# Moving half of the int4 compares to ScalarE and the mean-of-magnitudes sums to VectorE

## The reference, cut to what matters

```python
def simulate_quantize_int4(w):                 # layer 0, kernel: [1024, 1024]
    scale = jnp.max(jnp.abs(w)) / INT4_QMAX    # INT4_QMAX = 7.0
    q = jnp.clip(jnp.round(w / scale), -8.0, 7.0)
    return q * scale
...
def _quantize(W):                              # layer 1, W1 and W2
    gamma = jnp.mean(jnp.abs(W))
    return jnp.clip(jnp.round(W / (gamma + EPS)), -1.0, 1.0)
...
xn = _layernorm(x, axis=-1)
x = x + _L0_attn_ref(xn, ...) + _L0_ffn_ref(xn, kernel, bias, a, b)
xn = _layernorm(x, axis=-1)
x = x + _L1_attn_ref(xn, ...) + _L1_ffn_ref(xn, W1, b1, W2, b2)
```

## Time and profile before

| | us |
|---|---|
| median of 2 runs (1529.71 to 1533.32) | 1531.51 |
| the profiled execution | 1530.7 |
| its span on the slowest core, core 6 | 1529.2 |
| spans of the 8 cores | 1512.2 to 1529.2 |

### The profile page before, as it was taken

The page is one execution under the profiler, slowest core; times in us unless marked ns, Lnnn a source line. Parts: engine busy times, 40 slices in busy tenths (PEclk is TensorE's granted clock), DMA queues, the critical chain, the costliest instruction groups (busy, mean ns, idle before and its releaser), DMA issues. The chain is left out here.

```text
span 1529.2 us, 15301 instructions; the slowest of 8 cores (1512.2 to 1529.2 us)
## 1 busy us (share of the span) xinstructions
PE 1226.1 (80%) x5332; PEld 532.6 (35%) x5440; DVE 418.0 (27%) x704; ACT 474.2 (31%) x550; POOL 140.3 (9%) x184
## 2 busy tenths in 40 slices
PE   0277169999797587674559999999997999999997
PEld 0022024444343233221224444444443444444443
DVE  0498345002323323333167300030002200141000
ACT  0564023435424536626113241014102140032400
POOL 2341100000110211202200000000000000000000
PEclk9988679999898898896769999999998999999999
DMA  9796773002435637657592452355235152252432
GB/s 202 106 169 112 102 118 56 1 1 90 124 90 195 189 118 243 204 186 210 135 189 38 149 153 85 111 195 151 95 110 193 42 152 83 83 193 76 118 110 110
DMA packets 74202, 194.42 MB, mean 127 GB/s; under 512 B 8272, under 2 KB 16496, under 8 KB 69776
## 3 DMA queue, kind: packets, MB, share of 16 engines
q0 software_dynamic: 37072, 105.34, 28.4%
q1 hardware_dynamic: 37056, 88.09, 18.4%
HBM read 195.57 MB, written 33.56 MB: 150 GB/s over the span
## 5 line engine op out<-in xcount | busy, mean ns | idle before, releaser
L1217 PE MATMUL pb<-bigA,wqA 128*128 128x512 bf16 x1004 | 224.9, 379 | 1.1
L1177 PE MATMUL pb<-xn,xbf 128*128 128x512 bf16 x1004 | 221.4, 380 | 1.1
L1160 PE MATMUL pb<-stm,bigB 128*128 128x512 bf16 x626 | 146.2, 391 | 45.2 <-DVE xa_bf L1015 28.4
L1104 ACT ACTIVATE bigA<-pb,cstF 128x512 bf16<-128x512 f32 x128 | 99.5, 778 | 218.0 <-PE pb L1177 218.0
L1199 PE MATMUL pb<-rt,projW 128*128 128x512 bf16 x500 | 125.4, 391 | 43.8 <-DVE rt L1020 38.7
L1050 DVE SCALAR_TENSOR_TENSOR xf<-pb,cstF,xf 128x512 f32<-128x512 f32 x32 | 24.0, 750 | 479.6 <-PE pb L1217 479.6
L1177 PEld LDWEIGHTS pb<-xn,xbf 128*128 128x128 bf16 x1024 | 100.1, 98 | 121.8 <-issue 0.3
L1217 PEld LDWEIGHTS pb<-bigA,wqA 128*128 128x128 bf16 x1024 | 100.2, 98 | 120.8
L1160 PEld LDWEIGHTS pb<-stm,bigB 128*128 128x128 bf16 x640 | 63.0, 100 | 128.4 <-issue 59.5
L429 PE MATMUL pb<-rt,cstB 128*128 128x512 bf16 x110 | 34.5, 442 | 83.1 <-DVE rt L395 83.0
L1199 PEld LDWEIGHTS pb<-rt,projW 128*128 128x128 bf16 x512 | 48.2, 100 | 108.5 <-issue 58.7
(11 more groups left out here) (129 smaller groups left out, 1111.5 us busy)
## 6 DMA issues: line engine op xcount, KB each, us to landing
wqA<-W2qS POOLq DMA_DIRECT2D x32, 1024.0 KB, 5.1
xbf<-W1qS SPq DMA_DIRECT2D x128, 256.0 KB, 2.7
xbf<-W2T SPq DMA_DIRECT2D x26, 512.0 KB, 4.0
bigA<-W2T POOLq DMA_DIRECT2D x32, 256.0 KB, 9.2
bigA<-W1T POOLq DMA_DIRECT2D x16, 512.0 KB, 9.6
xf<-xT SPq DMA_DIRECT2D x4, 2048.0 KB, 8.2
x1S<-xf POOLq DMA_DIRECT2D x4, 2048.0 KB, 7.5
stm<-W1T SPq DMA_DIRECT2D x16, 512.0 KB, 5.5
```

The source lines that it names most:

```text
L1104: got = si(s.activation(bigA[:, fc * 512:(fc + 1) * 512], pb[fc % 2][:, :], AF.Relu, bias=biasL[:, 48 + fc:49 + fc], scale=sc[:, C_Q4:C_Q4 ...
L1160: got = ti(t.matmul(bank[:, :], bigB[:, i * 1024 + ec * 128: i * 1024 + (ec + 1) * 128], stm[:, i * 512:(i + 1) * 512], start=(n == 0), st ...
L1177: got = ti(t.matmul(bank[:, :], xbf[:, (fc % 4) * 1024 + dc * 128: (fc % 4) * 1024 + (dc + 1) * 128], xn[:, p0:p0 + TS], start=(dc == 0), ...
L1217: got = ti(t.matmul(bank[:, :], wqA[:, (dc % 2) * 4096 + fc * 128: (dc % 2) * 4096 + (fc + 1) * 128], bigA[:, fc * 512:(fc + 1) * 512], st ...
```

## The change

Of the 14 thresholds of a quarter, VectorE keeps the 7 even ones. The 7 odd ones go to ScalarE as Sign with a scale and a bias out of memory, giving 1 or -1. TensorE multiplies those by a new matrix `idH` of one half on the diagonal, and the eviction subtracts 3.5 in place of 7, since each sign is short by one half. ScalarE's 32 magnitude sums move to VectorE as a sum-reduction with absolute value, 8 units after each quarter's eviction. GpSimd now waits for VectorE's reductions (`v_gam`), and does its step with the maxima at u = 4 rather than 8. Seven threshold columns `thrC` are set by memset, and the constant `cblobB` grows from 384 to 512 columns.

```diff
             for u in range(NU):
-                if u == 8:
+                if u == 4:
                     g.wait_ge(sV, v_comb)
...
                 if u >= 4:
-                    g.wait_ge(sS, s_tok[u - 4])
+                    g.wait_ge(sV, v_gam(u - 4))
...
         def _(s):          # ScalarE
-            for u in range(NU):
-                s.wait_ge(gam4_q(u)[1], q_gm[u])
-                slot = (u % 4) * 2048
-                s.drain()
-                got = si(s.activation(
-                    bigA[:, 8192:8192 + 2048], bigA[:, slot:slot + 2048], AF.Abs,
-                    accum_out=statsT[:, u:u + 1]))
-                assert got == s_tok[u]
+            s.wait_ge(sV, v_r0)
+            for qr in range(4):
+                s.wait_ge(kq_q[qr][1], q_mx[qr])
+                for mi in range(7):
+                    m = 2 * mi + 1
+                    ci = 14 * qr + m
+                    if ci >= 4:
+                        q2, m2 = divmod(ci - 4, 14)
+                        s.wait_ge(sT, t_grp(q2, m2))
+                    cslot = xbf[:, (ci % 4 // 2) * 2048:(ci % 4 // 2) * 2048 + 2048]
+                    s.drain()
+                    got = si(s.activation(cslot, kq_slot(qr), AF.Sign,
+                                          scale=sc[:, C_R0:C_R0 + 1],
+                                          bias=thrC[:, mi:mi + 1]))
...
         def _(v):          # VectorE
             for qr in range(4):
-                for m in range(14):
+                for mi in range(7):
+                    m = 2 * mi
                     ci = 14 * qr + m
...
                     got = vi(v.tensor_scalar(
                         wqA[:, qr * 2048 + h * 512: qr * 2048 + (h + 1) * 512],
-                        pb[h][:, :], -7.0, sc[:, C_S0:C_S0 + 1], ALU.add, ALU.mult))
+                        pb[h][:, :], -3.5, sc[:, C_S0:C_S0 + 1], ALU.add, ALU.mult))
                 assert got == v_qev[qr]
-            v.wait_ge(sS, s_tok[NU - 1])
+                for k in range(8):
+                    u = 8 * qr + k
+                    v.wait_ge(gam4_q(u)[1], q_gm[u])
+                    v.drain()
+                    got = vi(v.reduce_sum(statsT[:, u:u + 1],
+                                          bigA[:, (u % 4) * 2048:(u % 4) * 2048 + 2048],
+                                          axis=AX.X, apply_absolute_value=True))
+                    assert got == v_gam(u)
+            v.drain()
...
         def _(t):          # TensorE
-                    t.wait_ge(sV, v_cmp(ci))
...
+                    if m % 2 == 0:
+                        t.wait_ge(sV, v_cmp(ci))
+                        lhsk = idP
...
+                    else:
+                        t.wait_ge(sS, s_sgn(ci))
+                        lhsk = idH
```

More of the change, by code:

```diff
@@ L61, in build_nc @@
     nmB = din("nmB", [128, 2048])
-    cblobB_in = din("cblobB", [128, 384], BF16)
+    cblobB_in = din("cblobB", [128, 512], BF16)
     outT = nc.dram_tensor("outT", [D, T], F32, kind="ExternalOutput").ap()
@@ L99, in build_nc @@
     projW = sb("projW", [128, 8192], BF16)
-    cstF = sb("cstF", [128, 2672], F32)
+    cstF = sb("cstF", [128, 2680], F32)
     Bcs = cstF.ap()[:, 0:512]
@@ L104, in build_nc @@
     sc = cstF.ap()[:, 2640:2672]
-    cstB = sb("cstB", [128, 384], BF16)
+    thrC = cstF.ap()[:, 2672:2680]
+    cstB = sb("cstB", [128, 512], BF16)
     idP = cstB.ap()[:, 0:128]
@@ L108, in build_nc @@
     inv1024 = cstB.ap()[:, 256:384]
+    idH = cstB.ap()[:, 384:512]
     a_sb = sb("a_sb", [128, 128], BF16)
@@ L277, in v_cmp, with v_gam, s_sgn @@
             q, m = divmod(ci, 14)
[L278 to L281, removed]
+            assert m % 2 == 0
+            return v0 + 8 + 19 * q + m // 2 + 1
+        v_qev = [v0 + 8 + 19 * q + 11 for q in range(4)]
+        def v_gam(u):
+            return v0 + 8 + 19 * (u // 8) + 12 + (u % 8)
+        v_gred = v0 + 8 + 76 + 2
+        def s_sgn(ci):
+            q, m = divmod(ci, 14)
+            assert m % 2 == 1
+            return s0 + 3 + 7 * q + (m - 1) // 2 + 1
+        s_tok = [0] * NU
         def t_grp(q, m):
@@ L344, in _ @@
             si(s.activation(sc[:, C_ALPHA:C_ALPHA + 1], sc[:, C_LA:C_LA + 1], AF.Exp))
-            for u in range(NU):
-                s.wait_ge(gam4_q(u)[1], q_gm[u])
-                slot = (u % 4) * 2048
-                s.drain()
-                got = si(s.activation(
-                    bigA[:, 8192:8192 + 2048], bigA[:, slot:slot + 2048], AF.Abs,
-                    accum_out=statsT[:, u:u + 1]))
-                assert got == s_tok[u]
+            s.wait_ge(sV, v_r0)
[12 more added lines that the diff above has]
+                                          bias=thrC[:, mi:mi + 1]))
+                    assert got == s_sgn(ci)
         @blk.vector
@@ L361, in _ @@
             v.memset(sc[:, C_HALFP:C_HALFP + 1], 0.5)
+            for mi in range(7):
+                v.memset(thrC[:, mi:mi + 1], -THRS[2 * mi + 1])
             v.wait_ge(sQg, qg_c[0])
@@ L391, in _ @@
                         v.wait_ge(sT, t_grp(q2, m2))
-                    cslot = (rt[:, (ci % 4 // 2) * 2048:(ci % 4 // 2) * 2048 + 2048]
-                             if ci % 2 == 0 else
-                             xbf[:, (ci % 4 // 2) * 2048:(ci % 4 // 2) * 2048 + 2048])
+                    cslot = rt[:, (ci % 4 // 2) * 2048:(ci % 4 // 2) * 2048 + 2048]
                     got = vi(v.tensor_scalar(
@@ L422, in _ @@
                     ci = 14 * qr + m
-                    t.wait_ge(sV, v_cmp(ci))
-                    cslot = (rt[:, (ci % 4 // 2) * 2048:(ci % 4 // 2) * 2048 + 2048]
-                             if ci % 2 == 0 else
-                             xbf[:, (ci % 4 // 2) * 2048:(ci % 4 // 2) * 2048 + 2048])
+                    if m % 2 == 0:
+                        t.wait_ge(sV, v_cmp(ci))
+                        lhsk = idP
+                        cslot = rt[:, (ci % 4 // 2) * 2048:
+                                   (ci % 4 // 2) * 2048 + 2048]
+                    else:
+                        t.wait_ge(sS, s_sgn(ci))
+                        lhsk = idH
+                        cslot = xbf[:, (ci % 4 // 2) * 2048:
+                                    (ci % 4 // 2) * 2048 + 2048]
                     got = None
                     for h in range(4):
-                        got = ti(t.matmul(pb[h][:, :], idP[:, :],
+                        got = ti(t.matmul(pb[h][:, :], lhsk[:, :],
                                           cslot[:, h * 512:(h + 1) * 512],
@@ L1323 @@
          rep(L1_attn_decay), rep(L1_attn_log_alpha)], axis=1)
-    cblobB = np.concatenate([idP, idN, inv1024], axis=1)
+    idH = (np.eye(128) * 0.5).astype(ml_dtypes.bfloat16)
+    cblobB = np.concatenate([idP, idN, inv1024, idH], axis=1)
     shared = {
```

## The result

The changed kernel takes 1606.18 us (median of 9 runs), against 1533.01 us for the kernel before (median of 8 runs of the same comparison). The ratio is 1.0483, with a 95% interval of 1.0462 to 1.0504: 73 us slower, where 1605 us in a range of 1591 to 1619 had been said. Two of the eight runs and one of the nine were in a slower state of the chip that shows now and then whatever the kernel; the ratio is of the others.

What follows compares the result with a forecast made beforehand. VectorE was taken to bound the first block: compares start at 56.8 us, four quarters of 42.0 (20.8 + 21.2) end at 224.8, final sums come 74.6 later than before; added to 1530.7 this gives 1605.3, said as 1605, range 1591 to 1619.

Steps and rivals of the forecast that it cites:

- The place: Only the first block, up to 163.9 us, changes in length; the 1365.3 us behind it stay as they are.
- VectorE's bill: VectorE in the first block: 32 reductions at 2.38 us add 76 us, 28 compares removed save 33.6; 43 us worse off.
- The compare part: Each quarter, first compare to end of eviction: 20.8 us, where the old quarter took 20.75.
- half of the time is TensorE at its low clock: Compare part: halving VectorE's compares gives back nothing; half of the time is TensorE's low clock, half ScalarE's signs.
- The reduction part: Each quarter after the eviction: eight reductions in a row on VectorE, beside them only loads; 21.2 us, bounds 19.0 and 22.
- Loads in time: Rival on the reductions after each eviction: no load late, 8 x 2.38 = 19.0 us a quarter, total 1596; chance 0.11.
- The head: From VectorE's maximum at 44.38 us to the first compare, said to come at 56.8 us, 10.1 sooner than before.
- 6.57 from there to the first compare: Last term before the first compare: from GpSimd's read-back to that compare, 6.57 us as in the kernel before.
- Quick reduction: Rival on VectorE's reductions: 1.28 us each on 16-bit data, 4 x 2.0 us less, total 1597; chance 0.06.
- long drain: Rival on GpSimd's drain ahead of the first compare: it stays at 9.7 us, 6.3 more, total 1612; chance 0.08.
- low clock throughout: Rival on TensorE in the compares: its clock stays low, 28.0 us for that part, 7.2 x 4 more, total 1634; chance 0.04.
- VectorE alone: Rival on the first block: VectorE's own work sets it, signs and loads never late, 30.1 us a quarter, total 1558; chance 0.02.

Runs made afterwards that it cites:

- filler run: Changed kernel plus filler matmuls of 512 columns into unused banks on TensorE while VectorE does the reductions; 1605.1 us, ratio 1.0457.
- six-slot pair: Kernel before with six unit slots in place of four and GpSimd's step at u = 6: unit 6 held back until the read-back landed, 1531.7 us; not held, 1527.4.
- five slots: Kernel before with five unit slots in place of four and GpSimd's step with the maxima at u = 5, nothing held back; 1527.4 us, ratio 0.9968.
- step at u = 6: Kernel before with GpSimd's step with the maxima at u = 6 instead of u = 8; 1529.2 us, one execution.
- six slots: Kernel before with six unit slots in place of four and GpSimd's step at u = 6, unit 6 not held back; 1527.4 us, ratio 0.9973.
- the kernel without loads: Changed kernel without its 32 reductions and without any unit's load, a constant standing in for the sums; 1509.1 us, one execution.

## Why the prediction was right

**The place.** Right: on core 6 the rest is 1365.5 against 1365.3 us.

**VectorE's bill.** Right: 2.286 us for a reduction (2.28 said). The row of the same operation on float32 was the right one, and the lower bound, the compare's 1.28 us, was not reached. The rule that the prediction cited from the Trainium skill, page "VectorE: DVE Perf Modes", section "The perf-mode tier table", that this operation has only its base rate, agrees with 2.286 us for bfloat16 and 2.280 for float32.

**The compare part.** 20.8 us said, 19.7 to 20.8 measured. A sign is 2.093 (2.09 said), and signs run back to back from the moment TensorE's first groups are through. What was a little off is the clock: it rose 3.3 us after the first group in the first quarter of core 6 and 5.0 in the second (92.23 to 97.25), where one quarter's 6.3 had been taken for all. The filler run prices what it costs in all, 2 us a quarter. So "half of the time is TensorE at its low clock" was too much: the clock was at 0.50 until 4 to 7 us into the part of 20, and ScalarE's signs set the rest.

**The reduction part.** 21.2 said, 19.0 to 22.7 measured. The waits came at another place: none ahead of the fifth unit, which landed within 7.2 us of its slot's freeing where 7.88 was taken, and about 1.4 us ahead of each of the next three. The sum of the two parts, four quarters, was 168.0 said and 168.2 on core 6, 166.2 on the mean. "Loads in time" held on core 3 alone.

**The head.** Off by 3.3 us: 12.6 said, 9.3 measured on the mean. The drain was 1.7 to 4.0 us, 2.8 on the mean, where 3.4 was taken. The term that was mis-sized is the "6.57 from there to the first compare": the read-back was carried over as if it cost the same, and it took 3.5 us on core 6 (44.73 to 48.23). Two things lie in the 3.1 us. One is the choice of core: in the kernel before, the way from the read-back to the first compare took 6.5 to 6.7 us on four cores, core 6 among them, and 3.5 to 4.0 on the other four. The other, 1.4 us on the mean of the cores (5.16 to 3.72), goes with the unit transfers: before, six to eight were issued right behind the read-back, now none are, and the six-slot pair shows the same 1.4 us.

**The total.** 1605 said, 1606.2 measured, and part of that closeness is luck. The profiled execution's slowest core, core 1, had its first compare at 47.5 us, 9.3 sooner than said: 3.0 of it are the head and 6.3 constants and loads that were there earlier. Its block was 169.7, 1.7 longer; its tail 2.2 shorter than core 6's of before; and behind the block it took 1373.8 us, 8.5 more than the 1365.3 that was assumed to stay. On core 6, where like is compared with like, the change cost 66.7 us where +74.6 was said.

**VectorE's and ScalarE's totals.** 455 and 466 us said, 460 and 469 measured. The sum took each compare off at its 1.28 us; they start 1.20 apart and overlap, so each had counted 1.20. Likewise the short read-outs of the accumulator, which went with the magnitude sums, had partly overlapped these.

**The rivals.** Quick reduction, long drain and low clock throughout did not show. "VectorE alone" was built, by another order: 30.1 us a quarter said, 30.0 measured, 1558 said, 1560.5 measured. What the prediction did not say is that the early step by itself, in which it saw 10 us, is worth only 4 in the kernel before, as the sums of magnitude then end last.

## What to carry to other kernels

Before moving work off an engine, ask who sets the stretch once it is gone: seven of fourteen compares left VectorE and the part shrank by less than 1 us, as TensorE at its low clock and ScalarE's signs were right behind. Work that is hidden on a second engine costs its full length when it is put in a row on the engine that sets the pace, and an in-order engine should get it between its own waits: the same instructions in another order were 46 us faster. A step that drains GpSimd is shortest where none of its transfers is in flight, but the loads that then come later must not end last: here that trade left 4 of 13 us.

## What the runs showed of the hardware

- GpSimd's drain has two parts that had not been expected. With units in flight it ended 1.11 us (five slots), 1.19 (step at u = 6, six slots) or 1.35 (the kernel before) after ScalarE had begun on the last of them. With none in flight it grows with the number of transfers that GpSimd has issued since its last drain. At the block's end it took 0.75 us with no unit transfers (two kernels), 3.38 with 32, 3.70 with 36, 3.87 with 38, 4.03 with 40: 0.75 + 0.082 for each. It cost the changed kernel 0.65 us there. The drain ahead of the compares agrees: 1.09 us in the kernel without loads, and 1.73 at the least with eight unit transfers more. So the 3.38 that the prediction carried over from the block's end was the price of 32 transfers. Core 6 of the changed kernel, with 40:

```profile
216.84 0.46 POOL L325 CROSS_LANE_REDUCE cstF<-cstF 128x2 f32<-128x2 f32 x1 [10.27 <-DVE cstF L434]
221.33 0.53 POOL L168 DMA_DIRECT2D bncS<-cstF  x1 [4.03 <-issue]
```

- From the issue of a read-back of 512 bytes to the first compare it is 3.5 us on most cores and at most 4.5 with no unit load behind it (six kernels, 48 cores). With unit loads issued right behind it (five kernels, 40 cores) it is 3.5 to 4.0 us on half of the cores and 5.7 to 6.8 on the other half. What parts the two halves stays open.
- TensorE's first group at the high clock came 3.3 us (core 6, first quarter of the changed kernel) in one place and 6.3 us in another after the first group of a quarter, and the longer times did not go with the longer pauses: 4.6 us of idling had the 6.3, and 27.0 us (core 6, second quarter) had 5.0. What decides it stays open.
